# Graph attention layer with residual norm: z2 turned in 32x32 blocks on VectorE and moved by sixteen on-chip transfers per row, instead of turned on TensorE

## Chip, cores and metric

One core of a Trainium2 chip runs the whole kernel. The metric is device time in microseconds of one execution; the time given for a kernel is the median of several runs. The engines are TensorE (PE, with its weight loads as PEld), VectorE (DVE), ScalarE (ACT), GpSimd (POOL) and SyncE (SP, which only issues transfers here).

## What is computed

3327 nodes with 512 features each, `x`, and a 0/1 adjacency matrix `adj` of 3327 x 3327, both float32. The reference, cut to what matters:

```python
sum_ = adj @ x
attn_a = sigmoid(concatenate([sum_, x], 1) @ Wa.T + ba)     # one number per node
attn_b = sigmoid(concatenate([sum_, x], 1) @ Wb.T + bb)
h = x @ W_sa
scores = (h @ a_sa[0, :D])[:, None] + (h @ a_sa[0, D:])[None, :]
e = where(adj != 0, exp(-leaky_relu(scores, 0.01)), 0)
x_a = e / (e.sum(1, keepdims=True) + 1e-5) @ h
x_b = adj @ (x @ W_gcnb) + b_gcnb
out = layernorm(x + sigmoid(attn_a * x_a + attn_b * x_b))
```

The kernel uses (e @ x) @ W_sa for e @ h and (adj @ x) @ W_gcnb for adj @ (x @ W_gcnb). It calls the first inner product z1 and the second, adj @ x, z2.

## The kernel before

The nodes are padded to 26 tiles of 128 rows. A "row" t below is one such tile of output (t = 0 to 25, LAST = 25), a "block" b is four rows (the last, b = 6, has two). Every float32 operand of a large product is split in two parts, hi and lo, so that three matmuls (hi hi, lo hi, hi lo) stand for one product, two where the other side is 0/1. x_hi and x_lo lie in SBUF for the whole kernel.

z1 of a block is summed over 26 source tiles j. For each pair g = 26 b + j, ACT makes the exponential (`steep`), DVE masks it with the adjacency tile (`weights`, line 737, three operations with lines 746 and 749), ACT makes e_hi (line 391), DVE e_lo (line 749), and PE does 12 matmuls of 128x512 (`sum_z1`, lines 570 to 572) into banks 0 to 3. e_hi and e_lo have rings of three, so DVE can be at most three steps ahead of PE. z1 comes out with features on the partitions, which is what the projection wants.

z2 of rows 0 to 3 is summed during block 0 of z1 (`sum_first`, lines 581 and 582); that of a later row t in seven chunks of up to four source tiles (`sum_z2`, lines 595 and 596) during row t - 2. Its adjacency chunks come through a ring of four buffers, `adj_r`, loaded by the GpSimd queue (`load_adj_r`, line 344): chunk m + 4 is issued when chunk m has been used. z2 comes out with nodes on the partitions. It has to be turned: `turn` (line 614) does four 128x128 PE transposes from z2s, ACT's copy of z2, into the PSUM bank `turned`; ACT copies that to zt_hi (`z2_hi`, line 445), DVE makes zt_lo (`z2_lo`, line 809), PE projects (`project_z2`, 12 matmuls on lines 619 to 621).

`places()` lays out the main loop. Block b of z1 (b = 1 to 6) is summed while rows t = 4 (b - 1) + q, q = 0 to 3, are finished; a row has 7, 6, 7 and 6 steps i of one z1 tile each (in block 6, whose steps are 256 columns wide, 9, 9, 8 and 0). All engines walk the same list, each with its own work at each step i:

- PE: i = 0 turn of row t; one chunk of z2 for row t + 2 in each step from row 2's sums on (so none in rows 0 and 1); 12 matmuls of z1; i = 1 `project_z2(t - 1)`; i = 4 `project_z1(t)`.
- DVE: the three `weights` operations; then i = 0 `z2_lo(t - 1)` and, at q = 0, `denominators`; i = 1 `add_bias`, `normalise(t - 2)`; i = 2 `gate_parts(t + 1)` (line 757 joins x_hi and x_lo into the one buffer x_row, two dots on line 713 read it) and `make_gates(t)`; i = 3 `z1_lo(t)` and a second join; i = 4 `add_p2`, `gate_dots`; i = 5 `residual`.
- SP: in each step the adjacency tile for the step three later (`load_adj`, line 237, waits until DVE has masked the current one); i = 2 the store of row t - 2.

Rows 24 and 25 follow after the loop in an order written out by hand, with z1 of both already in e_hi and e_lo. There PE does: wait for z2_lo(23), turn(24), chunk 4 of row 25 (`LAST_FIRST`), project_z2(23), projections of row 24, chunks 5 and 6, half of project_z1(25), turn(25), the other half, and 24 matmuls of 256 columns for z2 of row 25.

Of the kernel before, what the change touches and what calls it, by code (L numbers as in the profile page):

```python
# [7 lines left out]
F32 = mybir.dt.float32  # L8
# [3 lines left out]
P = 128  # L12
# [11 lines left out]
ADJ_R_RING = 4  # L24
EARLY_L = 9
# [3 lines left out]
def adj_resnorm_kernel(nc, x, adj_t, w_sa, w_sa_t, a_sa, w_gcnb, b_gcnb, wa, ba, wb, bb, out):  # L29
    TILES, _, D = x.shape  # L30
    KT = D // P
# [64 lines left out]
    with ExitStack() as ctx:  # L96
# [3 lines left out]
        def sem(name):  # L100
# [15 lines left out]
        adj_r = [sb(f"adj_r{s}", [P, CHUNK, P], F32R) for s in range(ADJ_R_RING)]  # L116
        l_row = sb("l_row", [P, WIDE * P])
# [32 lines left out]
        a_wide = [t[:, :].rearrange("p (k m) -> p k m", k=KT) for t in (l_row, esum)]  # L150
        diag = x_row[:, :].rearrange("p (q i) -> p q i", q=WIDE)
# [28 lines left out]
            sem(n) for n in ("row_up_ready", "den_ready", "denoms", "inverses", "alpha_ready"))  # L180
        turn_done, zt_hi_ready, zt_lo_ready, proj_done = (
# [31 lines left out]
        HALVES = (slice(0, D // 2), slice(D // 2, D))  # L213
        last_p2 = (bank[3], bank[0])
# [5 lines left out]
        def _(sp):  # L220
# [20 lines left out]
            def store(t):  # L241
                sp.wait_ge(y_ready, t + 1)
                sp.dma_start(out[t], y[:, t % 2, :]).then_inc(stored[t % 2], 16)

# [33 lines left out]
            for b, q, t, i, j, chunks in places():  # L278
                if j is not None:
                    load_adj(b * TILES + j + ADJ_RING)  # L280
                if i == 2 and t >= 2:
                    store(t - 2)
                if i == 3 and q == 3 and b < LASTB:
                    t0, n = (b + 1) * WIDE, width(b + 1)
                    sp.wait_ge(l_dot, t0 + n)
                    sp.dma_start(l_dram[b + 1, 0:n].rearrange("q p -> p q"), l_col[:, t0:t0 + n],
                                 allow_slow_non_contiguous=True) \
                        .then_inc(l_saved, 16)
# [72 lines left out]
        def _(act):  # L361
# [47 lines left out]
            def copy_z2(n):  # L409
                act.wait_ge(adj_r_used, sums_done(n))  # L410
                since(act, turn_done, n - 1)
                since(act, z_dots, 2 * (n - 1))
                if n < 2:
                    act.wait_ge(lo_ready, PIECES - 4)
                nc.scalar.copy(z2s[:, n % 2, :], sum_bank(n)[:, :]).then_inc(z2_copied, 1)
# [26 lines left out]
            def z2_hi(t):  # L442
                act.wait_ge(turn_done, t + 1)
                act.wait_ge(proj_done, 2 * t + 1)
                nc.scalar.copy(zt_hi[:, :, :].rearrange("p k i -> p (k i)"), turned[:, :]).then_inc(zt_hi_ready, 1)  # L445
# [76 lines left out]
            act.wait_ge(turn_done, LAST)  # L522
# [11 lines left out]
            act.wait_ge(turn_done, LAST + 1)  # L534
# [12 lines left out]
        def _(pe):  # L547
# [117 lines left out]
            for b, q, t, i, j, chunks in places():  # L665
                if i == 0:
                    since(pe, zt_lo_ready, 2 * t)
                    turn(t, turned)
                    if q == 0 and b > 1:
                        pe.wait_ge(denoms, b)  # L670
                for c in chunks:
                    sum_z2(chunk_number(t + 2, c))
                if j == TILES - 2 and b < LASTB:
                    sum_e(b)
                if j is not None:
                    sum_z1(b * TILES + j)
                if i == 1 and t >= 1:
                    project_z2(t - 1)
                if i == 3 and t == LAST - 2:
                    sum_e(LASTB)  # L680
                if i == 4:
                    project_z1(t)

            pe.wait_ge(zt_lo_ready, 2 * (LAST - 1))
            turn(LAST - 1, turned)
            sum_z2(chunk_number(LAST, LAST_FIRST))
# [18 lines left out]
        def _(dve):  # L705
# [55 lines left out]
            def gate_parts(n):  # L761
                since(dve, x_dots, 2 * n)
                since(dve, l_dot, min(max(n + 7, EARLY_L), TILES))
                join(n)
                for g in range(2):
                    dot(x_row[:, :], w_gate[:, g, 1, :], gate_bias[:, g:g + 1], gate_x[:, n, g:g + 1], x_dots,
                        2 * n + g + 1)
# [38 lines left out]

            def z2_lo(t):
                dve.wait_ge(zt_hi_ready, 2 * t + 2)
                nc.vector.tensor_tensor(zt_lo[:, :, :].rearrange("p k i -> p (k i)"), turned[:, :],  # L809
                                        zt_hi[:, :, :].rearrange("p k i -> p (k i)").bitcast(F32),  # L810
                                        ALU.subtract).then_inc(zt_lo_ready, 1)
# [111 lines left out]
            for b, q, t, i, j, chunks in places():  # L923
                if j is not None:
                    weights(b * TILES + j)
                if i == 0:
                    if t >= 1:
                        z2_lo(t - 1)
                    if q == 0:
                        denominators(b - 1)  # L930
# [52 lines left out]
            root(LAST - 1)  # L983
            normalise(LAST - 2)
# [4 lines left out]
            normalise_last(LAST - 1)  # L989
# [4 lines left out]
            for n, half in enumerate(HALVES):  # L994
                dve.wait_ge(proj_done, LAST_Z1[LAST] + n + 1)
# [5 lines left out]
            spread(LAST, last_stats[:, :, :].rearrange("p n s -> p (n s)"), LAST + 2)  # L1001
            root(LAST)
# [41 lines left out]
```

## Time and profile before

| | |
|---|---|
| three runs | 958.56, 958.62, 959.55 us; median 958.62 |
| profiled execution | 959.82 us, of which the span of instructions is 958.0 us |
| busy, share of span | PE 99%, PEld 82%, DVE 70%, ACT 37%, POOL 21% |
| DVE by fortieths of the span | 9 tenths in the first slices, 6 to 8 in slices 4 to 9, then 5 to 7 |
| granted TensorE clock, mean | 0.997 |
| moved by DMA | 108.97 MB, mean 114 GB/s |

Times are microseconds from the start of the span unless marked ns. A timeline row has start, duration, engine, line, operation, output and inputs; a bracket at its end is the idle time of the engine before it and who ended it. PE's matmuls overlap in the timeline, so the distance between their starts says what each costs. A group row has busy time, the mean of one instruction in ns, then the idle time before the group. SPq and POOLq are issues of transfers.

### The profile page before, as it was taken

How to read it: one execution, taken by the hardware profiler on the slowest of the kernel's cores; microseconds unless marked ns; L12 is line 12 of the kernel's file. 1: busy time of each engine (PE TensorE's matmuls, PEld its weight loads, DVE VectorE, ACT ScalarE, POOL GpSimd, SP SyncE). 2: the span in 40 equal slices, each digit the busy share in tenths (PEclk: the TensorE clock that was granted, in tenths of full speed). 3: DMA queues.
4: the chain of work that ended last, by engine and by line, in shares of the span. 5: the costliest groups of instructions: out<-in, count | busy, mean ns of one | idle time of the engine just before them, and what ended most of it. 6: DMA issues, size and time to landing. Idle time of an engine off the chain costs nothing.

```text
span 958.0 us, 12642 instructions
## 1 busy us (share of the span) xinstructions
PE 943.7 (99%) x4368; PEld 784.1 (82%) x4368; DVE 672.8 (70%) x1264; ACT 356.2 (37%) x618; POOL 199.1 (21%) x508
## 2 busy tenths in 40 slices
PE   9999999999999999999999999999999999999996
PEld 6888887788888888888888888888888888889875
DVE  6997868976676577577577577576576575566656
ACT  4564444442443242343332433342442342434312
POOL 3111100221221221221221221221221220222132
PEclk9999999999999999999999999999999999999999
DMA  9788632335433435433435333345344334343320
GB/s 283 193 212 209 178 103 77 94 99 106 120 94 105 110 94 116 110 94 105 111 95 116 109 95 106 108 106 115 99 107 114 93 112 87 84 121 89 87 63 33
DMA packets 139551, 108.97 MB, mean 114 GB/s; under 512 B 10336, under 2 KB 113632, under 8 KB 139488
## 3 DMA queue, kind: packets, MB, share of 16 engines
q1 hardware_dynamic: 102720, 62.42, 22.2%
q0 software_dynamic: 35904, 44.31, 21.8%
q10 hardware_dynamic: 864, 1.44, 0.8%
q8 instruction: 34, 0.56, 0.2%
q14 instruction: 29, 0.24, 0.1%
HBM read 101.32 MB, written 6.83 MB: 113 GB/s over the span
## 4 chain that ended last, share of the span: by engine, by line
PE 93%; DVE 2%; issue 2%; ACT 1%; POOL 1%; DMA 1%; SPq 0%; DVEq 0%; POOLq 0%; ACTq 0%
PE bank L570 15%; PE bank L572 15%; PE bank L571 15%; PE bank L595 14%; PE bank L596 14%; PE bank L619 4%; PE bank L620 4%; PE bank L621 4%; PE bank L581 2%; PE bank L582 2%; PE bank L614 1%; DMA w_gate<-w_sa_t_dram 1%; PE bank L607 1%; PE bank L553 0%; ACT e_hi L391 0%
## 5 line engine op out<-in xcount | busy, mean ns | idle before, releaser
L570 PE MATMUL bank<-e_hi,x_hi 128*128 128x512 f32 (+1 forms) x728 | 273.2, 375 | 1.4 <-DVE e_lo L749 1.1
L572 PE MATMUL bank<-e_lo,x_hi 128*128 128x512 f32 (+1 forms) x728 | 272.3, 374 | 0.0
L571 PE MATMUL bank<-e_hi,x_lo 128*128 128x512 f32 (+1 forms) x728 | 272.2, 374 | 0.0
L391 ACT ACTIVATE e_hi<-u,c_col 128x512 fp32r<-128x512 f32 (+1 forms) x182 | 126.1, 693 | 331.8 <-DVE u L737 215.7
L344 POOL DMA_DIRECT2D adj_r<-adj_t_dram x180 | 103.9, 578 | 660.5 <-PE bank L596 545.3
L595 PE MATMUL bank<-x_hi,adj_r 128*128 128x512 f32 x572 | 226.0, 395 | 0.0
L596 PE MATMUL bank<-x_lo,adj_r 128*128 128x512 f32 x572 | 223.8, 391 | 0.0
L749 DVE SCALAR_TENSOR_TENSOR e_lo<-u,c_col,e_hi 128x512 fp32r<-128x512 f32 (+1 forms) x182 | 129.9, 714 | 53.9 <-ACT e_hi L391 44.7
L570 PEld LDWEIGHTS bank<-e_hi,x_hi 128*128 128x128 f32 x728 | 137.0, 188 | 27.4 <-DVE e_lo L749 1.9
L571 PEld LDWEIGHTS bank<-e_hi,x_lo 128*128 128x128 f32 x728 | 137.0, 188 | 24.9
L572 PEld LDWEIGHTS bank<-e_lo,x_hi 128*128 128x128 f32 x728 | 137.0, 188 | 24.6
L383 ACT ACTIVATE u<-l_row,r_col 128x512 f32<-128x512 f32 (+1 forms) x182 | 126.2, 694 | 62.9 <-DVE e_lo L749 62.2
L746 DVE SCALAR_TENSOR_TENSOR esum<-u,c_col,esum 128x512 f32<-128x512 f32 (+1 forms) x175 | 124.9, 714 | 6.2
L596 PEld LDWEIGHTS bank<-x_lo,adj_r 128*128 128x128 f32 x572 | 108.1, 189 | 21.6
L595 PEld LDWEIGHTS bank<-x_hi,adj_r 128*128 128x128 f32 x572 | 108.0, 189 | 21.5
L737 DVE SCALAR_TENSOR_TENSOR u<-adj,u 128x512 f32<-128x512 f32 (+1 forms) x182 | 117.7, 647 | 1.7 <-DMA adj<-adj_t_dram 0.9
L804 DVE TENSOR_TENSOR zt_lo<-z1s,zt_hi 128x512 fp32r<-128x512 f32 x24 | 16.6, 692 | 85.6 <-ACT zt_hi L431 85.6
L619 PE MATMUL bank<-w_hi,zt_hi 128*128 128x512 f32 x196 | 76.4, 390 | 0.0
L620 PE MATMUL bank<-w_lo,zt_hi 128*128 128x512 f32 x196 | 76.3, 389 | 0.0
L621 PE MATMUL bank<-w_hi,zt_lo 128*128 128x512 f32 x196 | 76.3, 389 | 0.0
L809 DVE TENSOR_TENSOR zt_lo<-bank,zt_hi 128x512 fp32r<-128x512 f32 x24 | 16.6, 692 | 60.9 <-ACT zt_hi L445 60.9
L431 ACT CAST zt_hi<-z1s 128x512 fp32r<-128x512 f32 x24 | 14.9, 620 | 90.0 <-PE bank L621 90.0
(119 smaller groups left out, 838.5 us busy)
## 6 DMA issues: line engine op xcount, KB each, us to landing
adj_r<-adj_t_dram POOLq DMA_DIRECT2D x158, 256.0 KB, 3.2
adj<-adj_t_dram SPq DMA_DIRECT2D x156, 256.0 KB, 3.1
out_dram<-y SPq DMA_DIRECT2D x24, 256.0 KB, 3.8
z1s<-x_dram SPq DMA_DIRECT2D x14, 256.0 KB, 6.0
adj<-adj_t_dram SPq DMA_DIRECT2D x26, 128.0 KB, 2.4
adj_r<-adj_t_dram POOLq DMA_DIRECT2D x22, 128.0 KB, 2.9
z2s<-x_dram SPq DMA_DIRECT2D x6, 256.0 KB, 8.3
y<-x_dram SPq DMA_DIRECT2D x6, 256.0 KB, 5.2
```

Source lines behind the costliest of these rows:

```text
L383: nc.scalar.activation(u[g % U_RING][:, 0:cols(b)], l_row[:, 0:cols(b)], ACT.Exp, bias=r_col[:, j:j + 1]).then_inc(exp_done, 1)
L391: nc.scalar.activation(e_hi[g % E_RING][:, 0:cols(b)], u[g % U_RING][:, 0:cols(b)], ACT.Copy, scale=c_col[:, j:j + 1]).then_inc(e_hi_ready, 1)
L570: nc.tensor.matmul(z1[k][:, 0:n], x_hi[:, j, kk], e_hi[s][:, 0:n], start=(j == 0), stop=False)
L571: nc.tensor.matmul(z1[k][:, 0:n], x_lo[:, j, kk], e_hi[s][:, 0:n], start=False, stop=False)
L572: ins = nc.tensor.matmul(z1[k][:, 0:n], x_hi[:, j, kk], e_lo[s][:, 0:n], start=False, stop=(j == TILES - 1))
L595: nc.tensor.matmul(sum_bank(t)[:, :], adj_r[s][:, k, :], x_hi[:, j, :], start=(j == 0), stop=False)
L596: ins = nc.tensor.matmul(sum_bank(t)[:, :], adj_r[s][:, k, :], x_lo[:, j, :], start=False, stop=(j == TILES - 1))
L619: nc.tensor.matmul(into[:, half], hi(k), w_hi[:, h, k, half], start=(k == 0), stop=False)
L620: nc.tensor.matmul(into[:, half], hi(k), w_lo[:, h, k, half], start=False, stop=False)
L737: nc.vector.scalar_tensor_tensor(w, adj[g % ADJ_RING][:, 0:width(b), :].rearrange("p t i -> p (t i)"), 0.0, w, ALU.not_equal, ALU.min).the ...
L746: nc.vector.scalar_tensor_tensor(esum[:, 0:n], w, c, esum[:, 0:n], ALU.mult, ALU.add) \
L749: nc.vector.scalar_tensor_tensor(e_lo[s][:, 0:n], w, c, e_hi[s][:, 0:n].bitcast(F32), ALU.mult, ALU.subtract).then_inc(e_lo_ready, 1)
```

## The change

PE no longer turns z2 of rows 0 to 23. In step 0 of row t DVE turns z2s in 32x32 blocks with one operation into x_row (`turn_blocks`, after `z2_lo(t - 1)` and before `denominators`). In step 1 SP, after its adjacency load, waits for that and issues sixteen transfers (`move_blocks`), each of 32 partitions by four runs of 32 floats (16 KB), which carry the blocks to their partitions in a new buffer z2t. ACT and DVE then split z2t instead of the PSUM bank. x_row is the buffer that `gate_parts` joins into, so `gate_parts(t + 1)` in step 2 gets a wait for the transfers. z2t takes the room of one `adj_r` buffer: that ring goes from four to three. Rows 24 and 25 are still turned on PE. In the tail, chunk 4 of row 25 goes ahead of turn(24), and on DVE `root(24)`, `normalise(23)` and `normalise_last(24)` go behind work of row 25. The diff, cut by declarations and by the renumbered `turn_done` waits of the tail:

```diff
@@ -21,7 +21,7 @@
-ADJ_R_RING = 4
+ADJ_R_RING = 3
@@ -114,6 +114,7 @@
+        z2t = sb("z2t", [P, KT, P])
@@ -148,6 +149,7 @@
+        z2_blocks = x_row[:, :].rearrange("p (k m i) -> p k m i", k=KT, m=4)
...
+        blocks_turned, z2_moved = sem("blocks_turned"), sem("z2_moved")
...
+        MOVES = 16 * 16
@@ -241,6 +245,15 @@
+            def move_blocks(t):
+
+                sp.wait_ge(blocks_turned, t + 1)
+                since(sp, zt_lo_ready, 2 * t)
+                for a in range(4):
+                    for m in range(4):
+                        sp.dma_start(z2t[32 * m:32 * m + 32, :, 32 * a:32 * a + 32],
+                                     z2_blocks[32 * a:32 * a + 32, :, m, :]).then_inc(z2_moved, 16)
@@ -278,6 +291,8 @@
             for b, q, t, i, j, chunks in places():
                 if j is not None:
                     load_adj(b * TILES + j + ADJ_RING)
+                if i == 1:
+                    move_blocks(t)
                 if i == 2 and t >= 2:
                     store(t - 2)
@@ -408,7 +423,8 @@
             def copy_z2(n):
                 act.wait_ge(adj_r_used, sums_done(n))
-                since(act, turn_done, n - 1)
+                if n >= 2:
+                    act.wait_ge(blocks_turned, n - 1)
@@ -440,9 +456,9 @@
             def z2_hi(t):
-                act.wait_ge(turn_done, t + 1)
+                act.wait_ge(z2_moved, MOVES * (t + 1))
                 act.wait_ge(proj_done, 2 * t + 1)
-                nc.scalar.copy(zt_hi[:, :, :].rearrange("p k i -> p (k i)"), turned[:, :]).then_inc(zt_hi_ready, 1)
+                nc.scalar.copy(zt_hi[:, :, :], z2t[:, :, :]).then_inc(zt_hi_ready, 1)
...
@@ -663,11 +679,8 @@
             for b, q, t, i, j, chunks in places():
-                if i == 0:
-                    since(pe, zt_lo_ready, 2 * t)
-                    turn(t, turned)
-                    if q == 0 and b > 1:
-                        pe.wait_ge(denoms, b)
+                if i == 0 and q == 0 and b > 1:
+                    pe.wait_ge(denoms, b)
@@ -681,9 +694,9 @@
+            sum_z2(chunk_number(LAST, LAST_FIRST))
             pe.wait_ge(zt_lo_ready, 2 * (LAST - 1))
             turn(LAST - 1, turned)
-            sum_z2(chunk_number(LAST, LAST_FIRST))
             project_z2(LAST - 2)
@@ -761,6 +774,7 @@
             def gate_parts(n):
                 since(dve, x_dots, 2 * n)
                 since(dve, l_dot, min(max(n + 7, EARLY_L), TILES))
+                since(dve, z2_moved, MOVES * min(n, LAST - 1))
                 join(n)
@@ -804,10 +818,16 @@
+            def turn_blocks(t):
+
+                dve.wait_ge(z2_copied, t + 1)
+                since(dve, x_dots, 2 * t + 2)
+                since(dve, l_dot, min(max(t + 9, EARLY_L), TILES))
+                nc.vector.transpose(x_row[:, :], z2s[:, t % 2, :]).then_inc(blocks_turned, 1)
+
             def z2_lo(t):
                 dve.wait_ge(zt_hi_ready, 2 * t + 2)
-                nc.vector.tensor_tensor(zt_lo[:, :, :].rearrange("p k i -> p (k i)"), turned[:, :],
-                                        zt_hi[:, :, :].rearrange("p k i -> p (k i)").bitcast(F32),
+                nc.vector.tensor_tensor(zt_lo[:, :, :], z2t[:, :, :], zt_hi[:, :, :].bitcast(F32),
                                         ALU.subtract).then_inc(zt_lo_ready, 1)
@@ -926,6 +946,7 @@
                     if t >= 1:
                         z2_lo(t - 1)
+                    turn_blocks(t)
@@ -980,18 +1001,18 @@
             gate_dots(LAST)
-            root(LAST - 1)
-            normalise(LAST - 2)
             dve.wait_ge(zt_hi_ready, 2 * LAST)
...
             make_gates(LAST)
-            normalise_last(LAST - 1)
+            root(LAST - 1)
...
             for n, half in enumerate(HALVES):
+                if n == 1:
+                    normalise(LAST - 2)
                 dve.wait_ge(proj_done, LAST_Z1[LAST] + n + 1)
@@ -999,6 +1020,7 @@
             spread(LAST, last_stats[:, :, :].rearrange("p n s -> p (n s)"), LAST + 2)
+            normalise_last(LAST - 1)
             root(LAST)
```

## Rows read from the trace of the kernel before

**Rows 1.** PE timeline: first matmul of steps 3 and 4, row 0.

```profile
141.43 0.50 PE L570 MATMUL bank<-e_hi,x_hi 128*128 128x512 f32 x1
...
145.57 0.50 PE L570 MATMUL bank<-e_hi,x_hi 128*128 128x512 f32 x1 [1.10 <-DVE e_lo L749]
```

**Rows 2.** VectorE timeline, row 0: mask of step 1, join, e_lo of step 3.

```profile
130.90 0.68 DVE L737 SCALAR_TENSOR_TENSOR u<-adj,u 128x512 f32<-128x512 f32 x1
...
136.42 0.68 DVE L757 TENSOR_TENSOR x_row<-x_hi,x_lo 128x512 f32<-128x512 f32 x1
...
140.63 0.75 DVE L749 SCALAR_TENSOR_TENSOR e_lo<-u,c_col,e_hi 128x512 fp32r<-128x512 f32 x1
```

**Rows 3.** VectorE timeline, row 1: mask, join, e_lo of step 4.

```profile
154.52 0.68 DVE L737 SCALAR_TENSOR_TENSOR u<-adj,u 128x512 f32<-128x512 f32 x1
...
159.57 0.69 DVE L757 TENSOR_TENSOR x_row<-x_hi,x_lo 128x512 f32<-128x512 f32 x1
...
169.62 0.75 DVE L749 SCALAR_TENSOR_TENSOR e_lo<-u,c_col,e_hi 128x512 fp32r<-128x512 f32 x1
```

**Rows 4.** PE timeline: step 4 of row 1, turn of row 2.

```profile
170.68 0.39 PE L570 MATMUL bank<-e_hi,x_hi 128*128 128x512 f32 x1
...
179.97 0.66 PE L614 MATMUL bank<-ident,z2s 128*128 128x128 f32 x4 [0.98 <-DVE zt_lo L809]
```

**Rows 5.** PE timeline, row 9: start us, duration us, engine, line, operation.

```profile
403.81 0.39 PE L619 MATMUL bank<-w_hi,zt_hi 128*128 128x512 f32 x1
...
430.78 0.39 PE L572 MATMUL bank<-e_lo,x_hi 128*128 128x512 f32 x1
...
433.30 0.40 PE L570 MATMUL bank<-e_hi,x_hi 128*128 128x512 f32 x1
```

**Rows 6.** Groups by shape: busy us, mean ns | idle before: VectorE candidates.

```profile
L839 DVE TENSOR_SCALAR y<-y,norm 128x512 f32<-128x512 f32 x24 | 13.1, 546 | 45.4 <-POOL norm L331 45.4
L809 DVE TENSOR_TENSOR zt_lo<-bank,zt_hi 128x512 fp32r<-128x512 f32 x24 | 16.6, 692 | 60.9 <-ACT zt_hi L445 60.9
```

**Rows 7.** SyncE queue timeline: a burst, and one issue on its own.

```profile
1.18 1.84 SPq L247 DMA_DIRECT2D w_gate<-w_sa_t_dram  x4
...
222.55 0.37 SPq L237 DMA_DIRECT2D adj<-adj_t_dram  x1
```

**Rows 8.** DMA issues: KB each, median us from issue to landing.

```profile
out_dram<-z1s SPq DMA_DIRECT2D x4, 128.0 KB, 1.8
...
l_rows<-l_col SPq DMA_DIRECT2D x5, 2.0 KB, 9.4
```

**Rows 9.** VectorE, then PE, row 21: mask, join, e_lo, PE step 3.

```profile
852.17 0.41 DVE L737 SCALAR_TENSOR_TENSOR u<-adj,u 128x256 f32<-128x256 f32 x1
...
856.18 0.69 DVE L757 TENSOR_TENSOR x_row<-x_hi,x_lo 128x512 f32<-128x512 f32 x1
...
859.92 0.48 DVE L749 SCALAR_TENSOR_TENSOR e_lo<-u,c_col,e_hi 128x256 fp32r<-128x256 f32 x1
...
867.39 0.28 PE L570 MATMUL bank<-e_hi,x_hi 128*128 128x256 f32 x1
```

**Rows 10.** PE timeline, last rows: two waits and what follows.

```profile
928.46 0.76 PE L614 MATMUL bank<-ident,z2s 128*128 128x128 f32 x4 [1.98 <-DVE zt_lo L809]
...
932.37 0.39 PE L619 MATMUL bank<-w_hi,zt_hi 128*128 128x512 f32 x1
...
947.96 0.39 PE L619 MATMUL bank<-w_hi,e_hi 128*128 128x256 f32 x1 [1.32 <-DVE e_lo L986]
```

**Rows 11.** Stage behind a wait: us, busy by engine; PEclk, DMA share, GB/s.

```profile
930.20:932.00 1.80, 1.80 (x5) 1.32 (x5) 1.73 (x5) 0.00 (x0) 0.00 (x0) 0.50 0.39 146
```

**Rows 12.** GpSimd timeline, landing (12 to 24 us), PE: chunk 4 issued, 3 used.

```profile
14.56 0.74 POOL L344 DMA_DIRECT2D adj_r<-adj_t_dram  x1 [9.21 <-PE bank L582]
...
adj_r<-adj_t_dram POOLq DMA_DIRECT2D x5, 256.0 KB, 5.4
...
18.68 0.39 PE L581 MATMUL bank<-x_hi,adj_r 128*128 128x512 f32 x1
```

More of the change, by code:

```diff
@@ L521, in _ @@
             gate_exps(LAST - 1)
-            act.wait_ge(turn_done, LAST)
+            act.wait_ge(turn_done, 1)
             act.wait_ge(proj_done, 2 * (LAST - 2) + 2)
@@ L533, in _ @@
             copy_z2(LAST)
-            act.wait_ge(turn_done, LAST + 1)
+            act.wait_ge(turn_done, 2)
             nc.scalar.copy(e_hi[2][:, :], z2[0][:, :]).then_inc(zt_hi_ready, 1)
```

## The prediction

> **What bounds the kernel now.** I read the page first: PE is busy 99% of the span and DVE 70%, and the chain that ended last runs nearly all of it through PE's matmuls, so the time is what PE's stream costs plus the few places where PE waits. Then I read PE's timeline over one row for the price of a turn; the end of each e_lo against the start of the z1 matmuls that read it, for how far DVE is ahead; SP's queue for the price of an issue; and the tail.
>
> The reader is to see two regimes. From row 2 to row 23 PE is paced by its own matmuls, and DVE is some 5 to 11 us ahead. In rows 0 and 1 PE has no z2 chunks, a step is 12 matmuls (2.7 us), and DVE is the pace: in step 3 of row 0 e_lo ends at 141.38 and PE starts on it at 141.43; before step 4 PE idles 1.10 us for e_lo [rows 1, 2]; in step 4 of row 1 it is 170.37 against 170.68 [rows 3, 4]. What the change puts on DVE is free in the first regime and paid in the second.
>
> **PE's turns.** From 403.81 to 430.78 lie 119 matmul starts, 0.2266 us apart. From 430.78, the last z1 matmul ahead of turn(9), to the first behind chunk 0 are 2.52 us for nine matmuls that should take 2.04: a turn costs PE 0.48 us, part of it in slower starts of the matmuls behind it (at the least it is the quarter of a matmul's columns four times, an estimate of 0.23) [rows 5]. 24 turns go, but not all are worth that. Turn(0) lies beside ACT's copies of z1, for which PE waits anyway; turn(1) lies in the DVE-paced rows. Turn(2) takes its wait of 0.98 with it, as that zt_lo is next wanted by project_z2, a step later: 1.46 [rows 4]. The other 21 give 21 x 0.48 = 10.1.
>
> **The transpose on DVE.** No row has one. Nearest are 0.546 us (one input) and 0.692 (two inputs) for 128x512 floats; with one input I take 0.6 [rows 6]. That ACT and DVE read z2t in SBUF and no longer PSUM I price at nothing: PE's own work covers both.
>
> **The sixteen transfers.** Four issues directly behind each other take 1.84 us, 0.47 from start to start; one on its own 0.37 [rows 7]. A plain transfer lands 1.8 us after its issue [rows 8]. From the first issue the set needs 15 x 0.47 + 1.8 = 8.85 us; the low end is 15 x 0.37 + 1.8 = 7.35. The high end has no row, since none has this shape (32 partitions of four runs); I set it at 0.6, 10.8. The bytes are no matter: 256 KB, as much as one adjacency load.
> The Trainium skill (DMA: Bandwidth & Descriptors, Rules for kernel authors) speaks against the shape: coalesce small transfers, since under 64 KB they are mostly overhead. The issue rows agree. The same page (Why small descriptors are slow) says that on-chip transfers are spared the penalty of small descriptors; no row here shows that.
>
> **The new wait.** gate_parts(t + 1) on DVE waits for all sixteen, and behind it are all later masks and e_lo. Ahead of them SP issues one adjacency load (some 0.4 to the next issue), which itself waits for the mask of step 1.
> Row 0: the transpose goes in ahead of that mask, which then ends at 131.58 + 0.6 = 132.2; first move 132.7; landed 141.5. The join of gate_parts started at 136.42 and now does at 141.6: DVE is 5.15 us late, and as nothing is in hand PE's step 3 is 5.15 late [rows 1, 2].
> Row 1, on a time line shifted by that: mask ends 155.8, first move 156.25, landed 165.1, join at 165.15 and not 159.57, 5.6 late [rows 3]. Before, DVE idled 1.6 us between steps 3 and 4, for zt_hi; now it runs on. So e_lo of step 4 is 5.6 - 1.6 = 4.0 late, of which 0.3 were in hand: PE 3.6 later [rows 3, 4]. In row 2 step 3 has 7.3 us in hand, of which 5 are used: nothing.
> Rows 3 to 19: 8 to 11 us in hand at step 3, a stall of 0 to 3: nothing. Rows 21 and 22 have short steps. Row 21: mask ends 853.2, first move 853.65, landed 862.5; the join is 6.35 late and e_lo of step 3 ends at 860.4 + 6.35 = 866.75, against PE at 867.39 less the saved turn, 866.9 [rows 9]. It just holds; I take 0.25 a row, 0.5. Row 23 waits 2.7 us on DVE, beside z1_hi that waits for PE anyway.
> SP is held some 7.5 us in each step 1; the adjacency load behind it is wanted three steps later, 8 us at the least, and the store of row t - 2 a row later.
>
> **The clock.** PE idled 1.98 us before 928.46, and behind it the granted clock was 0.50 of full (1.2 of 2.4 GHz) in the stage from 930.2: turn(24) and eight matmuls took 932.37 - 928.46 = 3.91 us instead of 0.48 + 1.81 [rows 10, 11]. PE will now idle about 5 us in row 0 and 2 to 4 in row 1. In row 0 the lost clock is hidden, as PE waits for DVE again in row 1. In row 1 it is not: 0 to 1.6, I take 1.0.
>
> **The ring of three.** Chunks 3 and 4 of the start now wait until chunks 0 and 1 are used. The load issued at 14.56 was chunk 4's and becomes chunk 3's. Loads of that stretch land 5.4 us after issue (median), so at about 20.0 for a use at 18.68 [rows 12]. Chunk 4's goes out 1.8 later and lands as its use, moved too, comes. PE is bound from there to the end of block 0: 1.3 us (0 to 1.7). Later a chunk is loaded three uses ahead, 13 us: nothing.
>
> **The tail.** Chunk 4 (1.81 us) fills PE's wait ahead of turn(24), idle time falls to 0.3 and the clock should stay up: project_z2(23) starts at 928.9 and not 932.37, 3.5 us [rows 10]. Before the last 24 matmuls PE waits 1.32 for e_lo(25), which stands behind root(24) and normalise(23) on DVE. Without them it can start when ACT's copy is there; but PE is 3.5 earlier by then and DVE's chain for row 24 not wholly so, which takes half back: 0.7. normalise_last(24), 0.7 us, lies in DVE's wait for GpSimd's power and costs 0.1. Together 4.1.
>
> **Sum.** +1.3 (ring) + 5.15 (row 0) + 3.6 (row 1) + 1.0 (clock) + 0.5 (rows 21, 22) - 1.46 - 10.1 (turns) - 4.1 (tail) = -4.1. The profiled execution took 959.82 around its span of 958.0, 1.2 above the median of the runs; it would become 955.7, and the median 958.62 becomes 954.5.
>
> **Rivals.** A, the wait hardly binds: 7.35 us a set. Rows 0 and 1 give back 1.5 each, rows 21 and 22 their 0.5, the clock holds (1.0), the start costs 0.3 and DVE wins 1.5 more where a landing is quicker: -11, 947.5. For it: the lone issue of 0.37. Against: the burst [rows 7].
> B, the issue is slower, and the time ends above before. Each 0.1 us more per issue is 1.5 more a set, paid in rows 0, 1, 21 and 22, the last two having no slack left: about 5.7 us. It turns at 0.47 + 0.072 = 0.54 us an issue; at 0.62 it gives 963. For it: no row has such a shape. Against: the issue time hardly depends on bytes, 0.37 for a load in 512 runs.
> C, small packets land late: l_rows, 512 runs of 4 bytes, takes 9.4 us [rows 8]. Were the 2048 runs of 128 bytes to take three times 8.85, DVE would stall past its lead in every row: 975 and more. Against: those runs are 32 times as long and stay on chip, which is where the page named above counts against C.
> D, the change does not do what it says: PE's slower starts behind a turn belong to the first chunk of a row and stay, and only 0.23 comes back: 21 x 0.25 = 5.3 less, 959.8.
>
> **Chances.** Forecast (951 to 959) 0.50; A 0.20; B 0.20; C 0.05; D 0.05. The range reaches from A to B at 0.6 us, 947.5 to 962.5. A measurement of this kernel tells 0.2%, 1.9 us, from no change: faster is under 956.7. Forecast gives 0.38 of that, A 0.20: 0.58. Same: 0.12 of the forecast, 0.06 of B, D: 0.23. Slower: 0.14 of B and C: 0.19.
>
> **What would show it.** Right: DVE transposes of about 0.6 us; x_row's join some 5 us late in rows 0 and 1, PE idle about 5 us before step 3 of row 0; moves starting 0.47 apart; a steady row 0.48 shorter; no PE idle over 0.5 us from row 2 to 23; the clock at full around 929. Wrong: moves closer than 0.42 or wider than 0.52 apart, the last landing over 2.2 us after its issue, PE waits over 1 us in rows 21 and 22, or a start of chunk 3 that does not move.

## The result and the profile after

The changed kernel takes 1016.11 us (median of 4 runs, 1011.69 to 1018.94) against 958.59 of before beside it: 1.059 of before (95% interval 1.056 to 1.062). The forecast was 954.5, its range 947.5 to 962.5. All kernels below are compared with runs of before on the same chip, whose medians were 958.6 to 960.1. The profiled execution is the fastest of the four, 1011.69 us; what its trace shows is 51.9 us more than before's profiled execution (959.82) and not the 57.5 between the medians.

First the core's line, with the span and the mean granted clock, and the page's busy times by engine. PE has 96 matmuls fewer, the turns, and is yet busy for 4.5 us more (943.7 before). What is new is idle time of PE, and matmuls behind it at a lower clock (before: clock 0.997).

```profile
core 0: 1009.8 us, clock 0.973
```

```profile
PE 948.2 (94%) x4272; PEld 784.5 (78%) x4272; DVE 687.8 (68%) x1288; ACT 355.2 (35%) x618; POOL 213.6 (21%) x508
```

Then the list of waits: who waited for what, us in total, times, longest.

```profile
DVE x_row L770 <- DMA z2t<-x_row: 149.5, 24, 10.5
...
ACT e_hi L406 <- DMA l_rows<-l_col: 30.4, 4, 8.8
...
PE bank L623 <- DVE esum L759: 24.6, 5, 8.3
PE bank L586 <- DVE e_lo L762: 22.1, 6, 8.9
```

DVE stands at its join for the transfers in every one of 24 rows, 6.2 us each. PE pays 22.1 us for e_lo, which was foreseen in kind, and 24.6 us in sum_e for esum, which was not. The second line, ACT waiting for the store of l, leads to that.

The new work in four views: the moves' issues (least, median and longest in ns), their landing (KB each, median us), the transpose (busy us, mean ns), and SP's queue (start, duration, line, count).

```profile
L255 SPq DMA_DIRECT2D z2t<-x_row x384: 585/601/1819, 133.4 to 971.3; - x192
```

```profile
z2t<-x_row SPq DMA_DIRECT2D x384, 16.0 KB, 2.3
```

```profile
L826 DVE STREAM_TRANSPOSE x_row<-z2s 128x512 f32<-128x512 f32 x24 | 16.9, 703 | 0.0
```

```profile
133.45 11.61 SPq L255 DMA_DIRECT2D z2t<-x_row  x16
...
166.61 10.93 SPq L255 DMA_DIRECT2D z2t<-x_row  x16
```

The transpose takes 0.70 us, not 0.6. Sixteen issues take 11.61 us in row 0, (11.61 - 0.60) / 15 = 0.73 from start to start, and 10.93 in row 1, 0.69, where 0.47 was assumed [rows 7]; over the 24 rows it is 0.64 to 0.73. A move lands 2.3 us after its issue where 1.8 was assumed. From the first move to the join row 0 takes 12.96 us (133.45 to 146.41) and row 1 12.30, not 8.85; from first issue to last landing the 24 sets take 11.5 to 13.6 us.

DVE in row 0 (start, duration, what; in brackets the idle time before it and what ended it), and PE at the two waits that answer to [rows 1] and [rows 4], with the clock between them:

```profile
132.32 0.68 DVE L750 SCALAR_TENSOR_TENSOR u<-adj,u 128x512 f32<-128x512 f32 x1
...
146.41 0.69 DVE L770 TENSOR_TENSOR x_row<-x_hi,x_lo 128x512 f32<-128x512 f32 x1 [8.57 <-DMA z2t<-x_row]
```

```profile
151.71 0.79 PE L586 MATMUL bank<-e_hi,x_hi 128*128 128x512 f32 x1 [8.87 <-DVE e_lo L762]
...
183.93 0.79 PE L586 MATMUL bank<-e_hi,x_hi 128*128 128x512 f32 x1 [4.76 <-DVE e_lo L762]
```

```profile
152.00:164.00 12.00, 12.00 (x42) 9.61 (x42) 11.42 (x20) 6.21 (x10) 0.00 (x0) 0.77 0.29 81
164.00:176.00 12.00, 12.00 (x54) 9.94 (x54) 6.16 (x9) 4.28 (x8) 0.00 (x0) 1.00 0.24 54
```

Behind the wait of 8.87 us the granted clock is 0.77 for 12 us, with 42 matmuls where the next 12 us, at full clock, have 54.

To see where the rest comes from I set the start of each row's first z1 matmul against that of before. This shift, in us:

| | row 0 | 1 | 2 | 3 | 4 | 7 | 8 | 11 | 12 | 15 | 16 | 19 | 20 | 22 | last matmul |
|---|---|---|---|---|---|---|---|---|---|---|---|---|---|---|---|
| changed kernel | 1.4 | 11.2 | 16.4 | 17.0 | 27.3 | 25.8 | 30.9 | 29.4 | 35.8 | 34.3 | 43.4 | 41.9 | 42.8 | 45.6 | 51.7 |

From row 4 to row 19 every row but the last of a block is 0.48 shorter. Row 9 shows why, the turn is gone: from the last z1 matmul ahead of row 9 to the first behind chunk 0 are now 2.04 us, against 2.52 [rows 5].

```profile
461.66 0.39 PE L588 MATMUL bank<-e_lo,x_hi 128*128 128x512 f32 x1
...
463.70 0.39 PE L586 MATMUL bank<-e_hi,x_hi 128*128 128x512 f32 x1
```

The losses stand in three places: rows 0 to 2 (+15.7), the last rows of the blocks, 3, 7, 11, 15 and 19 (+10.3, +5.1, +6.3, +9.1, +0.9), and the end from row 20 on (+8.9). The middle one was in no term. PE waits for esum there for 8.3, 3.7, 4.4, 7.1 and 1.1 us; behind each of the first four the row loses another 1.9 to 2.5 us, the saved turn allowed for, in matmuls that take longer or start further apart while the granted clock is low (0.86 on average from 262 to 290 us). The chain in row 3, from SP's queue over ACT and DVE to PE:

```profile
233.53 11.14 SPq L255 DMA_DIRECT2D z2t<-x_row  x16
...
249.46 0.37 SPq L241 DMA_DIRECT2D adj<-adj_t_dram  x1
249.87 0.51 SPq L301 DMA_DIRECT2D l_rows<-l_col  x1
```

```profile
260.26 0.72 ACT L406 ACTIVATE e_hi<-u,c_col 128x512 fp32r<-128x512 f32 x1 [8.41 <-DMA l_rows<-l_col]
```

```profile
253.61 0.75 DVE L759 SCALAR_TENSOR_TENSOR esum<-u,c_col,esum 128x512 f32<-128x512 f32 x1
261.01 0.75 DVE L762 SCALAR_TENSOR_TENSOR e_lo<-u,c_col,e_hi 128x512 fp32r<-128x512 f32 x1 [6.66 <-ACT e_hi L406]
...
264.53 0.75 DVE L759 SCALAR_TENSOR_TENSOR esum<-u,c_col,esum 128x512 f32<-128x512 f32 x1
```

```profile
265.43 1.84 PE L623 MATMUL bank<-one,esum 128*128 128x1 f32 x8 [8.33 <-DVE esum L759]
```

In step 3 of a block's last row SP stores l for the next block, behind an adjacency load that waits for DVE's stalled mask. The store lands 9.9 us after its issue here, 7 to 10 in the other blocks. ACT waits for it before it issues load_l, and its e_hi of the same step stands behind that issue. Then DVE is late, and sum_e (line 623, 607 in before) wants esum of the block's last step, which is two steps ahead of PE. In before that esum ended at 239.08 and PE came to sum_e at 239.92, so 0.8 us were in hand:

```profile
238.33 0.75 DVE L746 SCALAR_TENSOR_TENSOR esum<-u,c_col,esum 128x512 f32<-128x512 f32 x1
...
239.92 0.95 PE L607 MATMUL bank<-one,esum 128*128 128x1 f32 x8
```

Read the same way, the slack of before at the five block ends (rows 3, 7, 11, 15, 19) is 0.8, 2.2, 2.0, 0.8 and 3.6 us. The changed kernel loses most where it was 0.8, and least where it was 3.6.

### The profile page after: what moved, and what is told of

The parts are those of the page before. It is cut to its first block and busy times, and to the rows that moved or that the text cites. A ratio compares the mean times of both kernels' runs of the same rounds, so it can differ in the third digit from the quotient of the medians.

```text
span 1009.8 us, 12881 instructions
## 1 busy us (share of the span) xinstructions
PE 948.2 (94%) x4272; PEld 784.5 (78%) x4272; DVE 687.8 (68%) x1288; ACT 355.2 (35%) x618; POOL 213.6 (21%) x508
## 5 line engine op out<-in xcount | busy, mean ns | idle before, releaser
L586 PE MATMUL bank<-e_hi,x_hi 128*128 128x512 f32 (+1 forms) x728 | 278.8, 383 | 23.4 <-DVE e_lo L762 22.1
L588 PE MATMUL bank<-e_lo,x_hi 128*128 128x512 f32 (+1 forms) x728 | 276.6, 380 | 0.0
L587 PE MATMUL bank<-e_hi,x_lo 128*128 128x512 f32 (+1 forms) x728 | 276.5, 380 | 0.0
L611 PE MATMUL bank<-x_hi,adj_r 128*128 128x512 f32 x572 | 223.2, 390 | 0.0
L586 PEld LDWEIGHTS bank<-e_hi,x_hi 128*128 128x128 f32 x728 | 140.4, 193 | 52.0 <-DVE e_lo L762 24.7
L587 PEld LDWEIGHTS bank<-e_hi,x_lo 128*128 128x128 f32 x728 | 140.5, 193 | 25.6
L588 PEld LDWEIGHTS bank<-e_lo,x_hi 128*128 128x128 f32 x728 | 139.7, 192 | 25.4
L770 DVE TENSOR_TENSOR x_row<-x_hi,x_lo 128x512 f32<-128x512 f32 x43 | 29.6, 689 | 149.5 <-DMA z2t<-x_row 149.5
L346 POOL TENSOR_TENSOR scratch<-scratch,factor 128x1 f32<-128x1 f32 x120 | 44.8, 373 | 9.4
L635 PEld LDWEIGHTS bank<-w_hi,zt_hi 128*128 128x128 f32 x196 | 36.8, 188 | 11.5 <-DVE zt_lo L987 2.1
```

Source lines behind the costliest of these rows:

```text
L586: nc.tensor.matmul(z1[k][:, 0:n], x_hi[:, j, kk], e_hi[s][:, 0:n], start=(j == 0), stop=False)
L587: nc.tensor.matmul(z1[k][:, 0:n], x_lo[:, j, kk], e_hi[s][:, 0:n], start=False, stop=False)
L588: ins = nc.tensor.matmul(z1[k][:, 0:n], x_hi[:, j, kk], e_lo[s][:, 0:n], start=False, stop=(j == TILES - 1))
L611: nc.tensor.matmul(sum_bank(t)[:, :], adj_r[s][:, k, :], x_hi[:, j, :], start=(j == 0), stop=False)
L635: nc.tensor.matmul(into[:, half], hi(k), w_hi[:, h, k, half], start=(k == 0), stop=False)
```

## The experiments

### The store of l ahead of the transfers

```diff
+                if i == 0 and q == 3 and b < LASTB:
+                    t0, n = (b + 1) * WIDE, width(b + 1)
+                    sp.wait_ge(l_dot, t0 + n)
+                    sp.dma_start(l_dram[b + 1, 0:n].rearrange("q p -> p q"), l_col[:, t0:t0 + n],
...
                 if i == 1:
                     move_blocks(t)
...
-                if i == 3 and q == 3 and b < LASTB:
```

> The changed kernel, with SyncE's store of l_rows (once per block, in its last row) issued in step 0, ahead of the moves, instead of step 3. Theory L (late store): in rows 3, 7, 11, 15 and 19 the stall of VectorE for the moves pushes that store behind it, it takes some 10 us to land, ScalarE waits for it ahead of e_hi, VectorE's esum comes late and PE waits 24.6 us in five places. Then these waits fall to at most 2 us each, the granted clock rises, and the time falls from 1016 to 985 to 995. Rival D (VectorE's lateness alone makes esum late): the five waits stay above 15 us together and the time stays above 1005.

Measured: 990.59 us, 1.032 of before (1.031 to 1.034), 25.5 less than the changed kernel. PE's waits for esum fall from 24.6 to 3.5 us, those for e_lo stay at 24.2:

```profile
260.58 0.58 PE L623 MATMUL bank<-one,esum 128*128 128x1 f32 x4 [2.92 <-DVE esum L759]
```

So the late store costs 25 us beside the stalled DVE, and more than half of the loss is elsewhere.

### No wait of DVE for the transfers

```diff
-                since(dve, z2_moved, MOVES * min(n, LAST - 1))
...
-                nc.vector.transpose(x_row[:, :], z2s[:, t % 2, :])
+                nc.vector.transpose(z2s[:, t % 2, :], z2s[:, t % 2, :])
```

z2s is turned in place and the moves read it, so x_row is free at once. ACT's copy_z2 waits for the moves of two rows earlier instead, and DVE's transpose for the gate dots that read z2s.

> The changed kernel, with the 32x32 turn done in place in z2s instead of into x_row, so that gate_parts no longer waits for the moves; ScalarE's copy into z2s waits for them instead, a row later. SyncE still issues the same sixteen moves in step 1. Theory W (the wait of VectorE is what costs): x_row's join waits for nothing, PE's waits in rows 0 to 2 and 20 to 22 go, the l_rows store goes out about when it did before, and the time falls to 946 to 955, under the 958.6 of before. Rival Q (SyncE's queue, held 10 us per row, is what costs, through late adjacency loads and the late l_rows store): the time stays above 985. Between the two: l_rows still 1 to 3 us late at five block ends, some 5 to 10 us in all.

Measured: 962.93 us (956.56 to 966.02), 1.002 of before (1.000 to 1.005), 53 less than the changed kernel. PE's waits for e_lo are 1.3 us. Those for esum are still 9.1 in five, and ACT still waits 30.5 us for l_rows: the queue alone, without any stall of DVE, makes the store late enough to matter.

### Both undone

> The changed kernel with both undone causes at once: z2s turned in place, so that gate_parts waits for no transfer, and the store of l for the next block issued in step 0, ahead of the sixteen transfers. If the wait on DVE and the late store are all that the change costs, what stands over is the saved turns and the tail: with in_place at 962.9 and its jumps of 6.7, 1.7, 0.7, 2.4 and 0.9 us at the ends of blocks gone (about 12), it comes to 951 us (947 to 955), 0.992 of before, and PE waits for esum nowhere over 0.5 us. Rival: the queue of SP held for 11 us in every row also makes adjacency loads and stores late, and only half of the 12 comes back: 956 to 960, with waits of PE that trace back to adj on DVE.

Measured: 945.38 us (944.69 to 945.88), 0.986 of before (0.985 to 0.988). This beats both kernels. PE's waits in the list of waits show nothing in sum_e; before step 4 of row 0 it waits 1.1 us, as in before [rows 1]:

```profile
PE bank L586 <- DVE e_lo L762: 1.3, 2, 1.1
PE bank L586 <- ACT z1s L422: 1.3, 1, 1.3
```

The four kernels make a table of two causes:

| | store of l in step 3 | store of l in step 0 |
|---|---|---|
| DVE waits for the transfers | 1016.1 | 990.6 |
| it does not | 962.9 | 945.4 |

DVE's wait costs 53 or 45 us, the late store 25 or 18. SP issues the same sixteen transfers in all four. Where the 45 lie is read from the shifts of the profiled executions with the early store, with the wait against without it: 1.0 ahead of row 0, 17.5 in rows 0 to 2, 5.7 in row 3, 4.3 in the later ends of blocks, and 16.8 from row 20 on. The time was below the 951 that I expected; a likely reason, not tested, is that I had taken the block ends from the one profiled execution of in_place, which is low in its range (958.2 - 12.4 = 945.8).

### What an issue costs: one run a partition, two queues, four wide transfers, reads from device memory

```diff
-                        sp.dma_start(z2t[32 * m:32 * m + 32, :, 32 * a:32 * a + 32],
-                                     z2_blocks[32 * a:32 * a + 32, :, m, :])
+                        sp.dma_start(z2t[32 * m:32 * m + 32, a, :],
+                                     x_row[32 * a:32 * a + 32, m * P:(m + 1) * P])
```

> The changed kernel, with sixteen moves of the same 16 KB each and the same 32 partitions, but one run of 128 floats per partition instead of four of 32: it moves the wrong blocks, so z2 enters the projection scrambled, with all work and waits as they were. If the number of runs sets the 0.64 us from issue to issue, the moves start 0.40 to 0.50 apart, the set takes 9 us instead of 12, and the time falls to 975 to 995. If it is the on-chip transfer as such or its half-filled partitions, they stay 0.6 to 0.7 apart and the time stays within 1009 to 1020.

Measured: 1020.59 us, 1.063 of before (1.060 to 1.066). Sixteen in 10.95 us, landing 2.3: both as with four runs of 128 bytes a partition. The number of runs is not it. Beside this row the Trainium skill (DMA: Bandwidth & Descriptors, Why small descriptors are slow), which spares on-chip transfers the penalty of small descriptors, agrees: 2.3 us with runs of 128 bytes and 2.3 with runs of 512.

The next kernel gave the second half of the moves to ACT, which issues its eight in step 0 of the row as soon as the blocks are turned.

> The changed kernel, with eight of the sixteen moves issued by ScalarE in step 0 and eight by SyncE in step 1. If the set is bound by issuing, it takes 7 x 0.65 + 2.3 = 7 us instead of 12, and PE's wait in row 0 falls from 8.9 to 3 to 5 us; ScalarE's eight issues hold back its exponentials by about 5 us, so not all is won: 965 to 985. If the set is bound by the DMA engines (2048 runs of 128 bytes), it still takes 11 to 12 us and the time stays above 1005.

Measured: 1012.67 us, 1.055 of before (1.052 to 1.058). The two queues did run side by side, eight in 5.2 us on ACT's and eight in 5.1 on SP's. But ACT is held as long as it issues:

```profile
162.72 5.18 ACTq L521 DMA_DIRECT2D z2t<-x_row  x8
168.00 0.72 ACT L398 ACTIVATE u<-l_row,r_col 128x512 f32<-128x512 f32 x1 [6.66 <-issue]
```

Its exponentials wait 158.3 us for its own issues over the run, and PE waits 18.4 us for ACT's copies of z1, 13.9 for esum and 11.7 for e_lo. The expectation had the hold of 5 us, but not that it is paid in every row and comes between PE and the copies of z1 at the start of each block.

```diff
-                    for m in range(4):
-                        sp.dma_start(z2t[32 * m:32 * m + 32, :, 32 * a:32 * a + 32],
-                                     z2_blocks[32 * a:32 * a + 32, :, m, :]).then_inc(z2_moved, 16)
+                    sp.dma_start(z2t[:, :, 32 * a:32 * a + 32], z2_blocks[:, :, a, :])
```

> The changed kernel with four transfers of 128 partitions (64 KB each) in place of sixteen of 32 partitions (16 KB each): the same bytes, but the blocks keep their partitions, so z2's contribution is wrong; that part of the computation is changed. If an issue costs by the transfer, whatever its partitions: four in 2.5 us, all landed after 5, DVE's join late by nothing, the store of l late by 2.5 instead of 11: 950 to 957 us. Rival, an issue costs by the partitions (runs) that it names: 2.5 us each, the set takes the same 11 to 12 us, and the time stays at 1005 to 1018. Between them 0.9 to 1.2 us an issue: 955 to 970.

Measured: 947.97 us, 0.989 of before (0.988 to 0.990):

```profile
159.57 2.65 SPq L254 DMA_DIRECT2D z2t<-x_row  x4
```

(2.65 - 0.60) / 3 = 0.68 us from start to start, with four times the partitions and bytes. So what an issue costs here goes by the transfer and hardly by its size.

For the last one the moves of one_run read x[t] in device memory.

> What sets the 0.64 us between two issues? The sixteen transfers read 32 partitions x 128 floats of the input in device memory and no longer the turned row on chip, in the shape of one_run (issue 0.59 us, 16 KB), so z2's contribution is changed. If reading on chip is what makes an issue slow, they start 0.40 to 0.48 us apart like the loads of the kernel before, and the set lands after some 9 us; the time falls to 955 to 985. Rival: an issue with 32 partitions or 16 KB costs what it does wherever it reads: 0.64 apart and 1010 to 1020 us.

Measured: one run, 987.83 us, beside a before of 959.3. The issue is as fast as the loads of before:

```profile
163.75 7.40 SPq L255 DMA_DIRECT2D z2t<-x_dram  x16
```

(7.40 - 0.42) / 15 = 0.465 us. The same shape takes 0.69 when it reads on chip. So rival B's "no row has such a shape" was right in its result and wrong in its reason: it is where the transfer reads, not how many partitions or runs it names. The time is above the 985 at which my range ended, and that is the more useful half: with the very issue that the prediction assumed, and 8.87 us from first move to join in row 1 (the sets of all rows take 8.8 to 10.9, median 9.9), the kernel is 29 us slower than before.

### How the time goes with the length of the set

Eleven and eight transfers cover z2t in larger pieces; nothing else is changed but which blocks are moved and how many landings are waited for. The edit of eight (eleven cuts the first three m at k = 1 too):

```diff
+                for m in range(4):
+                    a = (m + 1) % 4
+                    for k0, k1 in ((0, 2), (2, 4)):
+                        sp.dma_start(z2t[32 * m:32 * m + 32, k0:k1, :],
+                                     x_row[32 * a:32 * a + 32, k0 * P:k1 * P])
```

> The changed kernel with eleven transfers of 32 partitions in place of sixteen, covering all of z2t (some of them 32 KB); the blocks come from the next 32 partitions, so z2's contribution is changed, and nothing else. At the measured spacing of 0.66 us the set takes 10 x 0.66 + 2.4 = 9.0 us from first issue to landing, which is the 8.85 that the prediction assumed for sixteen. If only the size of the set was wrong in the prediction, its sum holds here: 954.5 us (951 to 959). Rival: the store of l behind the held queue was left out of the sum and costs at this size too, at the ends of blocks: 962 to 985, with waits of PE for esum.

> The changed kernel with eight transfers of 32 partitions, 32 KB each, that cover all of z2t; as in the kernel with eleven, the blocks come from the next 32 partitions, so z2's contribution is changed. The set takes 7 x 0.66 + 2.4 = 7.0 us, near the 7.35 of rival A of the prediction (947.5). With four transfers of 128 partitions the time was 948.0. If the sum is right below the point where waits show, 948 to 951; if the late store of l already costs at this size, 953 to 962, with waits for esum.

Measured: eleven 973.73 us, 1.014 of before (1.011 to 1.017), with 9.6 us of waits for esum; eight 958.85, 1.000 (0.998 to 1.001), with 4.3. In order of DVE's total wait at the join:

| | issues | DVE's wait | time |
|---|---|---|---|
| four wide | 4 | 5.9 | 948.0 |
| eight | 8 | 32.5 | 958.9 |
| eleven | 11 | 65.5 | 973.7 |
| sixteen from device memory | 16 | 84.4 | 987.8 |
| changed kernel | 16 | 149.5 | 1016.1 |

The rival's range held for both, and PE waits for esum: at the size of set that the prediction took the ends of blocks already cost. That the store is the reason is for the next kernel to show.

Last, eleven transfers with the store in step 0, meant as the set that the prediction assumed without the effect that it left out.

> The kernel with eleven transfers (blocks from the next 32 partitions, so z2's contribution is changed), with the store of l for the next block in step 0, ahead of them. It has the set that the prediction assumed (8.6 to 9 us from first issue to landing) and not the effect that it left out. If these two are all that was wrong, its sum holds: 954.5 us (952 to 957), the shift at row 2 as with eleven (+9), then 0.48 less with every row, and no waits of PE for esum over 0.5 us. Rival: the wait of DVE in every row costs at the ends of blocks by itself, since DVE's lead is spent: 962 to 970.

Measured: 960.83 us, 1.001 of before (1.000 to 1.003). Neither theory: six more than the sum, and less than the rival's least by one. Its shift says where. It is 7.9 at row 2 where the sum had +1.3 + 5.15 + 3.6 + 1.0 - 1.46 = 9.6, falls by 0.48 a row as it should, but rises by 3.0 at row 3 (PE waits 1.67 for esum), and the end wins 0.5 instead of 4.6 (4.1 for the tail and 0.48 for the turn of row 23).

Row 3 shows that the kernel did not have the assumed set everywhere. With the store of l just ahead of them, its eleven moves take 14.1 us from first issue to last landing, where the same moves took 8.7 in eleven; in rows 7, 11 and 15 it is 11.5 to 11.9 for 8.2 to 8.4. DVE stands 8.53 us at that join:

```profile
222.18 8.41 SPq L256 DMA_DIRECT2D z2t<-x_row  x11
```

```profile
236.37 0.69 DVE L771 TENSOR_TENSOR x_row<-x_hi,x_lo 128x512 f32<-128x512 f32 x1 [8.53 <-DMA z2t<-x_row]
```

So moving the store ahead of the burst has a price of its own, and the 25 and 18 us above are what the move wins net of it. The same is seen with sixteen moves: row 3's set takes 12.4 us in the changed kernel and 14.5 in early_l.

At the end PE waits for y and zt_lo, and y traces back to the join in step 2 of row 23, where DVE waits 5.29 us for the moves:

```profile
922.91 0.69 DVE L771 TENSOR_TENSOR x_row<-x_hi,x_lo 128x512 f32<-128x512 f32 x1 [5.29 <-DMA z2t<-x_row]
...
926.19 0.75 DVE L844 SCALAR_TENSOR_TENSOR y<-bank,gates,y 128x512 f32<-128x512 f32 x1
```

```profile
927.08 0.47 PE L636 MATMUL bank<-w_hi,zt_hi 128*128 128x512 f32 x1 [1.62 <-DVE y L844]
```

Between that join and y DVE has no idle time here; in in_place_early_l, which has no such wait, it idles 2.59 us for zt_hi in the same place, and PE waits for neither.

### The tail alone, the ring alone

The edits are those of the diff for the last rows, and ADJ_R_RING = 3, each in the kernel before.

> The kernel before with the new order of the last rows alone (chunk 4 of row 25 ahead of turn(24) on PE; root(24), normalise(23) and normalise_last(24) put later on DVE). The prediction's term: 4.1 us less than before (2.5 to 4.5), PE starting project_z2(23) some 3.5 us earlier, and no granted clock of 0.50 behind PE's wait ahead of turn(24). Rival: what is won ahead of project_z2(23) is given back before the end, because DVE's chain for rows 24 and 25 is the pace there and nothing on it got shorter: 0 to 1.5 us less, with longer waits of PE for y, zt_lo or e_lo in the last 40 us.

Measured: 956.22 us, 0.997 of before (0.996 to 0.998), so 2.8 less (1.7 to 3.7; 2.4 by the medians). PE's wait ahead of turn(24) is 0.17 and not 1.98 [rows 10]:

```profile
929.28 0.66 PE L614 MATMUL bank<-ident,z2s 128*128 128x128 f32 x4 [0.17 <-DVE zt_lo L809]
```

> The kernel before with a ring of three for adj_r and nothing else. The prediction's term: 1.3 us more (0.3 to 1.7), from chunk 3 of the start landing at about 20.0 for a use at 18.68. Rival, from the trace of the changed kernel, where PE waits only 0.26 us for that load and z1 of row 0 starts 0.8 later in all: 0 to 0.8 more, too little to be told from no change; later waits for chunks none in either.

Measured: 959.44 us, 1.0009 of before (1.0001 to 1.0018), so 0.9 more (0.1 to 1.7). This kernel has before's tail, and it shows what was too large in the tail's term. The same wait of 1.98 us is there, and behind it the clock is full:

```profile
930.10 0.66 PE L614 MATMUL bank<-ident,z2s 128*128 128x128 f32 x4 [1.98 <-DVE zt_lo L809]
```

```profile
930.20:932.00 1.80, 1.80 (x11) 1.54 (x12) 1.18 (x3) 0.00 (x0) 0.94 (x3) 1.00 0.00 0
```

Eleven matmuls in the stretch in which before's profiled execution had five, at a clock of 0.50 [rows 11]. So the drop does not come with every execution that has this wait; how often it comes in before is not known from one profile of each. Its price is the shift that goes with it: ring_only is 1.64 us behind before ahead of this place and 0.04 behind after it, so 1.6 of the 4.1.

## Why the prediction was wrong

Set beside the sum, the profiled execution misses by 56 us (+51.7 in the last shift where the sum has -4.1). Of these 34 are in rows 3 to 19 (+25.8 for the sum's 17 x -0.48 = -8.2), 7.4 in rows 0 to 2 (+15.7 for 5.15 + 3.6 + 1.0 - 1.46 = 8.3), and 14.4 from row 20 on (+8.9 for 0.5 - 4 x 0.48 - 4.1 = -5.5).

**PE's turns: right.** 0.48 a row, wherever PE is bound by its own matmuls, so rival D falls. In in_place_early_l it holds from row 2 to row 20 without a gap (shift -1.4 at row 2, -10.1 at row 20). Row 2 gives 1.8 for the 1.46.

**The tail and the ring: right in kind, and over.** 2.8 for 4.1 and 0.9 for 1.3. Of the tail, 1.6 was a clock drop read from one execution and charged to every one; 4.1 - 1.6 = 2.5 is near the 2.8. With the ring, the turns and row 2 the sum without any wait is 958.6 + 0.9 - 1.46 - 10.1 - 2.8 = 945.1; in_place_early_l has 945.4. So with the ring and the tail as measured, all but the wait and the queue adds up.

**The sixteen transfers: mis-sized, the second failure.** 0.64 to 0.73 an issue, not 0.47, above even the high end of 0.6; 11.5 to 13.6 us a set, not 8.85. That is beyond the point at which rival B decides, and B was the right rival, but its price was not: 5.7 us for each 0.1 us puts 0.66 at 965, and the kernel stands at 1016.

**Rows 0 and 1: right, given the size.** With the issue that was assumed (from_dram) row 0 costs 6.4 for 5.15, and row 1 with the first turns and the clock 1.6 for 3.6 + 1.0 - 1.46 = 3.1: together 8.0 for 8.3. At the real size they are 9.8 and 5.2, and row 2 adds 0.6. The clock behind PE's wait fell as said, to 0.77 over 12 us. What the prediction had no term for is the clock behind the waits at the ends of blocks, 1.9 to 2.5 us each in rows 3, 7, 11 and 15.

**"Rows 3 to 19: 8 to 11 us in hand at step 3, a stall of 0 to 3: nothing": the step that failed.** The stall does not shrink with DVE's lead. The moves go out behind the mask of step 1, and from there to the join DVE has some 5 us of work, however early it is, and in some rows 1 to 3 us of other waits. At the assumed size the stall was right: in eleven it is 1.3 to 3.6 us in rows 3 to 19. At the real size it is 4.4 to 7.4 in these rows, 7.2 in row 9. At step 3 even that was borne. In row 9 PE's step 3 had 11.3 us in hand before (e_lo ended at 438.36, PE came at 449.63) and has 2.9 now (477.11 and 480.02). Before, then the changed kernel:

```profile
437.61 0.75 DVE L749 SCALAR_TENSOR_TENSOR e_lo<-u,c_col,e_hi 128x512 fp32r<-128x512 f32 x1
...
449.63 0.39 PE L570 MATMUL bank<-e_hi,x_hi 128*128 128x512 f32 x1
```

```profile
476.36 0.75 DVE L762 SCALAR_TENSOR_TENSOR e_lo<-u,c_col,e_hi 128x512 fp32r<-128x512 f32 x1
...
480.02 0.39 PE L586 MATMUL bank<-e_hi,x_hi 128*128 128x512 f32 x1
```

But I measured the lead only at e_lo against z1. The tightest consumer of DVE's lead is sum_e, which comes once a block, wants esum of a step that is two ahead, and had 0.8 us in hand in rows 3 and 15 and 2.0 to 3.6 in the other three. PE's waits there are 24.6 us, and rows 3 to 19 cost 34 us more than the sum had. At the assumed size of the set it is still 16.8 (eleven, +8.6 for -8.2), of which 13.3 go with the store in step 0 (eleven_early_l, -4.7); the 3.5 left are all in row 3, where that kernel's set took 14.1 us.

**"SP is held some 7.5 us in each step 1; the adjacency load behind it is wanted three steps later": incomplete in the same way.** I named the loads and the store of y behind the burst and not the third issue in that queue, the store of l, though its landing of 9.4 us stands in [rows 8], where I used it for another purpose. It costs 18 us with DVE free and 25 with DVE stalled.

**Rows 21 and 22: right at the assumed size; the end: wrong.** "It just holds" is what eleven_early_l shows: e_lo of step 3 ends 0.4 us ahead of PE in row 21 and 0.1 in row 22, PE waits over 0.3 us in neither, and rows 20 and 21 are each 0.48 shorter. At the real size PE waits 2.5 us in row 21 and 4.6 in row 22:

```profile
948.46 0.58 PE L586 MATMUL bank<-e_hi,x_hi 128*128 128x256 f32 x1 [4.60 <-DVE e_lo L762]
```

Rows 20 and 21 lose 2.8, and all from row 22 on 6.1. "Row 23 waits 2.7 us on DVE, beside z1_hi that waits for PE anyway" failed even at the assumed size: the stall is 5.3 us, its set takes 9.7, and in eleven_early_l the end is 3.9 us longer than in the kernel without the wait, 1.62 and 1.64 of them PE's waits for y and zt_lo. The first goes back to that join; the second I did not follow to its start, and no run takes the wait away in row 23 alone.

**What stays open.** From_dram and eleven are 14 us apart. In row 1 from_dram has the shorter set (8.9 and 9.7 us to the join), but over all rows it has the longer one (medians 9.9 and 8.8), and DVE's wait is 84.4 against 65.5. The steps up at the ends of blocks are larger in from_dram (7.3, 5.3, 6.0 and 6.3 for 4.8, 1.0, 2.9 and 5.4). Whether that is its longer wait alone or its reads of device memory beside the store was not tried, and from_dram is one execution.

## What to carry to other kernels

When a change puts a wait or a burst on an engine or a queue, list every consumer of that engine's lead and every issue behind the burst, the ones that come once a block above all, and look up how much each has in hand: the smallest slack sets the price, not the usual one. A new wait costs least where its buffer can be freed without it: turning in place and one store moved ahead of the burst took the same change from 6% slower to 1.4% faster. A clock drop seen once in one execution is a range, not a term.

## What the runs showed of the hardware that I had not expected

- An issue that reads on chip takes 0.63 to 0.68 us from start to start (medians of the changed kernel, one_run, four_wide, eleven and eight), with 32 partitions or 128, one run a partition or four, 16, 32 or 64 KB; the shape of one_run read from device memory takes 0.464.
- Moves issued right behind the store of l land later: eleven of them take 14.1 us in row 3 of eleven_early_l and 8.7 in eleven.
- The Trainium skill (DMA: Bandwidth & Descriptors, Rules for kernel authors) says to coalesce small transfers. The runs agree: four of 64 KB take 2.65 us of the queue, sixteen of 16 KB 10.9.
- Eight issues on SP's queue and eight on ACT's at once (two_queues) take 5.1 and 5.2 us, 0.64 and 0.65 from start to start, so neither queue slows the issues of the other; a move then lands 2.8 us after its issue, for 2.3 with one queue.
- The same wait of 1.98 us of PE was followed by a granted clock of 0.50 in one execution (before) and of 1.00 in another (ring_only).
- DVE's transpose of 128x512 floats in blocks of 32x32 takes 0.703 us, as long as an operation with two inputs.
